# Attention scores and sums on TensorE: products of both kinds dealt out one by one, half a unit later

## The reference

```python
q = conv1x1(wq, x).reshape(n, NH, HD, H, W)      # NH = 16 heads, HD = 16; k and v alike
qk = einsum('nhcij,nhciw->nhijw', q, k) / D      # D = 16
qrq = einsum('nhcij,chjw->nhijw', q, rq) / D
krk = einsum('nhcij,chjw->nhijw', k, rk) / D
weight = softmax(qk + Gq * qrq + Gk * krk, axis=3)
out = einsum('nhijw,nhciw->nhcij', weight, Gv1 * v) + einsum('nhijw,chjw->nhcij', weight, Gv2 * rv)
return conv1x1(wo, out)
```

## Time and profile before

| what | us |
|---|---|
| median of three runs | 8297.43 |
| the profiled execution | 8291.75 |
| its span, first to last instruction | 8290.0 |
| PE, mean granted clock over the span | 0.749 |
| POOL normalise (L787), mean of one | 1.934 |
| DVE add and largest (L737), mean of one | 0.286 |

### The profile page before, as it was taken

The page is one execution under the profiler, slowest core; times in us unless marked ns, Lnnn a source line. Parts: engine busy times, 40 slices in busy tenths (PEclk is TensorE's granted clock), DMA queues, the critical chain, the costliest instruction groups (busy, mean ns, idle before and its releaser), DMA issues. The chain is left out here.

```text
span 8290.0 us, 275612 instructions
## 1 busy us (share of the span) xinstructions
PE 7187.2 (87%) x106442; PEld 6044.4 (73%) x106442; DVE 5176.6 (62%) x20646; ACT 4856.3 (59%) x11427; POOL 2457.0 (30%) x1235
## 2 busy tenths in 40 slices
PE   4999999799999999999999899999999966766738
PEld 3555555689988888898899898898888932332338
DVE  5444444366666666666666666666666768988830
ACT  1444444577777777777777777777777733333410
POOL 0000000243443443444434444434434432322210
PEclk7999999666666666666666666666667688988855
DMA  7555555565655665655556656656656576766522
GB/s 217 203 203 204 204 204 197 113 112 100 112 103 98 113 107 101 107 99 107 101 106 112 102 100 109 109 99 110 105 100 109 92 232 203 265 201 202 208 74 99
DMA packets 1721071, 1148.11 MB, mean 138 GB/s; under 512 B 1143009, under 2 KB 1506145, under 8 KB 1703329
## 3 DMA queue, kind: packets, MB, share of 16 engines
q1 hardware_dynamic: 1530336, 842.56, 48.1%
q10 hardware_dynamic: 188352, 285.27, 9.3%
q0 software_dynamic: 1024, 2.09, 0.1%
HBM read 708.04 MB, written 421.56 MB: 136 GB/s over the span
## 5 line engine op out<-in xcount | busy, mean ns | idle before, releaser
L787 POOL TENSOR_TENSOR att_scores<-att_scores,att_inverse 128x1024 f32<-128x1024 f32 x1024 | 1966.8, 1934 | 2951.7 <-DVE att_inverse L722 2951.7
L660 ACT ACTIVATE att_scores<-att_scores,att_negmax 128x128 f32<-128x128 f32 x8192 | 2509.2, 399 | 67.6 <-issue 67.6
L737 DVE CUSTOM_DVE_ANT_0 att_scores<-att_ps,att_scores 128x128 f32<-128x128 f32 x8192 | 1780.8, 286 | 1066.7 <-PE att_ps L573 957.5
L560 PE MATMUL att_ps<-att_qk,att_rs 32*128 32x64 f32 x32768 | 1793.2, 380 | 155.6 <-ACT att_scores L652 114.2
L560 PEld LDWEIGHTS att_ps<-att_qk,att_rs 32*128 32x128 f32 x32768 | 1698.6, 299 | 196.2 <-ACT att_scores L652 142.5
L573 PE MATMUL att_ps<-att_own 16*128 16x128 f32 x16384 | 1541.6, 405 | 231.3 <-issue 224.1
L573 PEld LDWEIGHTS att_ps<-att_own 16*128 16x128 f32 x16384 | 1416.2, 300 | 268.9 <-issue 264.4
L652 ACT ACTIVATE att_scores<-att_ps 128x1024 f32<-128x1024 f32 x1024 | 992.4, 1021 | 1044.3 <-PE att_ps L560 1044.3
L720 DVE TENSOR_REDUCE att_total<-att_scores 128x8 f32<-128x1024 f32 x1024 | 1233.7, 1205 | 70.7 <-issue 70.7
L594 PE MATMUL att_ps<-att_scores,att_rv 128*16 128x64 f32 x32768 | 1249.6, 334 | 11.0 <-issue 10.8
L594 PEld LDWEIGHTS att_ps<-att_scores,att_rv 128*16 128x16 f32 x32768 | 1193.6, 127 | 24.5 <-issue 13.1
(11 more groups left out here) (146 smaller groups left out, 5276.0 us busy)
## 6 DMA issues: line engine op xcount, KB each, us to landing
qk<-proj_qk_out ACTq DMA_DIRECT2D x64, 2048.0 KB, 8.5
att_qk<-qk SPq DMA_DIRECT2D x512, 256.0 KB, 6.7
att_own<-qk SPq DMA_DIRECT2D x2048, 64.0 KB, 2.5
proj_x<-in_x_dram SPq DMA_DIRECT2D x128, 512.0 KB, 4.3
v_t<-proj_v_out ACTq DMA_DIRECT2D x64, 1024.0 KB, 11.3
att_vt<-v_t SPq DMA_DIRECT2D x128, 512.0 KB, 5.5
att_v<-att_att_v SPq DMA_DIRECT2D x512, 128.0 KB, 4.2
att_r<-att_att_r SPq DMA_DIRECT2D x512, 128.0 KB, 3.5
```

Source lines behind the costliest of these rows:

```text
L560: last = pe.matmul(ps[:, 4 + g, jj * IU:(jj + 1) * IU], rs[32 * g:32 * g + 32, t * JB + jj, :], qk[b][32 * g:32 * g + 32, :, t * JB + jj], ...
L660: last = act.activation(scores[v][:, i, :], scores[v][:, i, :], ACT.Exp, bias=negmax[v][:, i:i + 1], scale=-1.0)
L737: last = dve.tensor_tensor_reduce(out=scores[v][:, i, :], in0=ps[:, 2 * (p % 2) + r // 4, (r % 4) * W:(r % 4 + 1) * W], in1=scores[v][:, i ...
L787: pool.tensor_tensor(scores[v][:, rows, :], scores[v][:, rows, :], inverse[v][:, rows].unsqueeze(2).broadcast_to([P, PR, W]), ALU.mult).th ...
```

## The change

Only `attend` and constants above it are changed. In words:

- PE deals its products out one by one. A unit has four quarters. In each step a few own products, a few table products and a few sums follow each other.
- Everything is shifted by half a unit: in the first half of unit u the sums are those of the second half of unit u - 2, in the second half those of the first half of u - 1. In the last quarter the table products are round 0 of unit u + 2.
- Own scores come in 16 pieces of four image rows, two pieces (two row groups) together, in every second group of steps. They take 32 array rows instead of 16, of which the lower half is cleared once to zero. They use banks 0 and 1; the table products 2 to 5; sums with v bank 6; sums with rv bank 7.
- ACT no longer reads v; DVE reads all four fills. ACT and DVE follow with pieces of four rows; sums, inverses and normalising stay at eight rows.
- vt, att_v and att_r are halved into two buffers each, with their own semaphores; rv comes in four loads. Loads and stores are issued in halves or quarters. att_r is laid out in runs of 16 instead of 32 in DRAM, and `combine` reads it so.

```diff
-PR = 8
+PR = 4
 PIECES = IU // PR
+SR = 8
+SPIECES = IU // SR
-JT = JG
+JT = JG // 2
+STORES_G = JG // JT
...
+            def own_score(u, p, r):
+                half, g = p // (PIECES // 2), p % G
+                if r == 0:
+                    if p % (PIECES // 2) == 0:
+                        pe.wait_ge(own_loaded[half], 128 * u + 128)
+                    later(pe, added, PIECES * u + p - 1)
+                at = (p // G) % (HROWS // 16) * PR + r
+                last = pe.matmul(ps[:, p % 2, r * W:(r + 1) * W], own[half][32 * g:32 * g + 32, 1, at, :], own[half][32 * g:32 * g + 32, 0, at, :],
+                                 start=True, stop=True, tile_position=(32 * g, 0))
...
+            def unit(u, v, parts):
+                back2, back1, now, ahead1, ahead2 = parts
+                for q in range(4):
+                    rel_on, sums_on = (ahead1, ahead1, ahead1, ahead2)[q], (back2, back2, back1, back1)[q]
+                    ru, rt = (u + 1, q + 1) if q < 3 else (u + 2, 0)
+                    rb = v + 1 if q < 3 else v + 2
+                    su, sb, b = (u - 2, v - 2, q + 2) if q < 2 else (u - 1, v - 1, q - 2)
+                    for x in range(PR):
+                        if now:
+                            own_score(u, 4 * q, x)
+                            own_score(u, 4 * q + 1, x)
+                        if rel_on:
+                            relative(ru, rb, rt, range(3 * x, 3 * x + 3))
+                        if sums_on:
+                            sums_with_v(su, sb, b, range(2 * x, 2 * x + 2))
+                    for x in range(PR):
+                        if rel_on:
+                            relative(ru, rb, rt, range(12 + 3 * x, 15 + 3 * x))
+                        if sums_on:
+                            sums_with_v(su, sb, b, range(8 + 2 * x, 10 + 2 * x))
+                            sums_with_r(su, sb, b, range(2 * x, 2 * x + 2))
+                    for x in range(PR):
+                        if now:
+                            own_score(u, 4 * q + 2, x)
+                            own_score(u, 4 * q + 3, x)
+                        if rel_on:
+                            relative(ru, rb, rt, range(24 + 2 * x, 26 + 2 * x))
+                        if sums_on:
+                            sums_with_r(su, sb, b, range(8 + 2 * x, 10 + 2 * x))
+                    for x in range(PR):
+                        if sums_on:
+                            sums_with_r(su, sb, b, range(16 + 4 * x, 20 + 4 * x))
...
             def unit(u, v, parts):
                 back2, back1, now, ahead1, ahead2 = parts
+                for p in range(PIECES):
+                    if p < BEHIND:
+                        if back1:
+                            exp_piece(u - 1, (v - 1) % BUFS, PIECES - BEHIND + p)
+                    elif now:
+                        exp_piece(u, v, p - BEHIND)
+                    q = p // 4
+                    if p % 4 == 3:
+                        if q < 3 and ahead1:
+                            read_relative(u + 1, v + 1, q + 1)
+                        if q == 3 and ahead2:
+                            read_relative(u + 2, v + 2, 0)
+                        if q < 2 and back2:
+                            read_r(u - 2, q + 2)
+                        if q >= 2 and back1:
+                            read_r(u - 1, q - 2)
```

More of the change, by code:

```diff
@@ L512, in unit @@
                     load_qk(*after(h, k, 2))
-                fresh = left >= 2 and k == UPH - 2
+                if started >= 2:
+                    store(*before(h, k, 2), u - 2, 0)
+                if started >= 1:
+                    ph, pk = before(h, k, 1)
+                    later(sp, v_done, FILLS * (u - 2) + FILLS // 2)
+                    load_v(ph, pk, 0)
+                    if pk == 0:
+                        later(sp, r_done, FILLS * (u - 2) + FILLS // 2)
+                        load_rv(ph, 0)
+                        load_rv(ph, 1)
+                fresh = k == UPH - 2 and left >= 2
                 if fresh:
@@ L520, in unit @@
                     load_own(*after(h, k, 1), 0)
+                if started >= 1:
+                    later(sp, v_done, FILLS * (u - 1))
+                    load_v(ph, pk, 1)
+                    if pk == 0:
+                        later(sp, r_done, FILLS * (u - 1))
+                        load_rv(ph, 2)
+                        load_rv(ph, 3)
+                if started >= 2:
+                    store(*before(h, k, 2), u - 2, 1)
                 if fresh:
@@ L546, in _ @@
+            store(NH - 1, UPH - 2, UNITS - 2, 1)
+            for a in range(2):
+                store(NH - 1, UPH - 1, UNITS - 1, a)
+            for a in range(2):
+                sp.wait_ge(v_stored[a], 64 * UNITS)
+                sp.wait_ge(r_stored[a], 64 * UNITS)
         @block.tensor
         def _(pe):
[L548 to L596, removed]
@@ new lines, in relative @@
+            def relative(u, v, t, steps):
+                if 0 in steps:
+                    if t == 0:
+                        pe.wait_ge(qk_loaded[v % 2], 64 * (u // 2) + 64)
+                    if t % (ROUNDS // 2) == 0:
+                        pe.wait_ge(rs_ready[t // (ROUNDS // 2)], u // UPH + 1)
+                    later(pe, rel_read, ROUNDS * u + t)
+                for x in steps:
+                    jj, g = x // G, x % G
+                    last = pe.matmul(ps[:, 2 + g, jj * IU:(jj + 1) * IU], rs[32 * g:32 * g + 32, t * JB + jj, :],
+                                     qk[v % 2][32 * g:32 * g + 32, :, t * JB + jj], start=True, stop=True, tile_position=(32 * g, 0))
+                if JB * G - 1 in steps:
+                    last.then_inc(rel_done, 1)
@@ new lines, in sums_with_v @@
+            def sums_with_v(u, v, b, steps):
+                if 0 in steps:
+                    if b % (FILLS // 2) == 0:
+                        pe.wait_ge(v_loaded[b // (FILLS // 2)], 16 * u + 16)
+                    if b == 0:
+                        pe.wait_ge(normed, SPIECES * u + SPIECES)
+                    later(pe, v_read, FILLS * u + b)
+                for x in steps:
+                    r, g = x // G, x % G
+                    i = 16 * b + 4 * r + g
+                    last = pe.matmul(ps[32 * g:32 * g + HD, 6, r * W:(r + 1) * W], vt[i // HROWS][:, i % HROWS, :], scores[v % BUFS][:, i, :],
+                                     start=True, stop=True, tile_position=(0, 32 * g))
+                if 15 in steps:
+                    last.then_inc(v_done, 1)
@@ new lines, in sums_with_r @@
+            def sums_with_r(u, v, b, steps):
+                if 0 in steps:
+                    pe.wait_ge(rv_loaded[b], (u // UPH) * 16 + 16)
+                    later(pe, r_read, FILLS * u + b)
+                for x in steps:
+                    jj, g = x // G, x % G
+                    j = g * JG + b * JB + jj
+                    last = pe.matmul(ps[32 * g:32 * g + HD, 7, jj * IU:(jj + 1) * IU], rv[:, j, :], scores[v % BUFS][:, :, j],
+                                     start=True, stop=True, tile_position=(0, 32 * g))
+                if JB * G - 1 in steps:
+                    last.then_inc(r_done, 1)
@@ L640, in _ @@
+            pe.wait_ge(cleared, 3)
             for t in range(ROUNDS):
-                relative(0, 0, t)
+                relative(0, 0, t, range(JB * G))
+            relative(1, 1, 0, range(JB * G))
             units(pe, unit)
@@ new lines, in read_r, with unit @@
+            def read_r(u, b):
+                act.wait_ge(r_done, FILLS * u + b + 1)
+                if b % 2 == 0:
+                    later(act, r_stored[b // 2], 64 * u)
+                act.activation(att_r[b // 2][:, :, (b % 2) * JB:(b % 2 + 1) * JB], ps[:, 7, :].rearrange("p (j i) -> p i j", i=IU), ACT.Copy).then_inc(r_read, 1)
+            BEHIND = 2
+            def unit(u, v, parts):
+                back2, back1, now, ahead1, ahead2 = parts
+                for p in range(PIECES):
[14 more added lines that the diff above has]
+                            read_r(u - 1, q - 2)
@@ new lines, in _, with unit @@
+            BEHIND = 2
+            def unit(u, v, parts):
+                back2, back1, now, ahead1, ahead2 = parts
+                for p in range(PIECES):
+                    q = p // 4
+                    if now:
+                        add_and_largest(u, v, p)
+                    if p % 4 == 2 and q < 2 and back2:
+                        read_v(u - 2, q + 2)
+                    if p % 4 == 2 and q >= 2 and back1:
+                        read_v(u - 1, q - 2)
+                    if p % 2 == 1:
+                        k = p // 2 - BEHIND
+                        if k >= 0 and now:
+                            sums_of(u, v, k)
+                        elif k < 0 and back1:
+                            sums_of(u - 1, (v - 1) % BUFS, SPIECES + k)
@@ L773, in _ @@
+            for half in range(2):
+                dve.memset(own[half][:, :, :, :], 0.0).then_inc(cleared, 1)
```

(9 more changed lines are left out.)

221 lines of the change are left out of this document (53 added, 168 removed).

## The result

The changed kernel takes 11,529.76 us (median of 4 runs, 11,481.67 to 11,549.69) against 8,293.69: ratio 1.389, 95% interval 1.3845 to 1.3944. 12,700 was forecast: the change was to cost about 4,400 us and costs 3,236. All of it is in the attention stage.

The account below looks back on a forecast made before the run. PE (TensorE), busy 4,709 of attention's 5,086 us, was taken as the bound. 8,292 + 4,400 (74.1 us a unit, 128 units, half clock) + 40 for part units = 12,730, said as 12,700; 8 in 10: 8,200 to 13,400.

Parts of the forecast that it names:

- What a change of kind costs: On PE in attention, each switch between row and column products costs 0.09 us at full, 0.14 at half clock; 96 against 2.
- A: Quarter's section, four steps of 2 own, 3 table, 2 v products; step's rows 0.99 us, columns 0.56 at half clock.
- B: Quarter's section, four steps of 3 table, 2 v, 2 rv products; step's rows 0.57 us, columns 0.81 at half clock.
- C: Quarter's section, four steps of 2 own, 2 table, 2 rv products; step's rows 0.83 us, columns 0.39 at half clock.
- section D: Last section of a quarter on PE, 16 rv products in all, nothing but sums; 1.16 us at half clock.
- Rivals 2 and 3: Changes of kind cost nothing between short runs: 7,180 us in total (chance 0.17), or with the clock down 8,300 (0.06).
- The added wait: PE waits at each quarter's start for ACT to read four table banks: 0.8 us four times, 3.1 a unit.
- Which clock: PE in attention stays at half clock throughout: 74.1 us a unit, 9,485 us instead of 5,086, +4,400.
- What costs nothing: ACT and DVE work, smaller pieces, 32-row own scores, clearing, loads and combining add 0; part units at the ends about +40 us.
- the case of half of the time up: Rival: changes of kind cost as forecast, but full clock half of the time, about 11,100 us; chance 0.17 with clock always up.

Follow-up runs that it names:

- by section: The changed kernel with sections A, B and C of a quarter each making row products first, column products after (24 changes of kind a unit, not 96): 8,197 us, ratio 0.989.

## Why the prediction was right, and where it was not

- **What a change of kind costs: right.** It was read off three seams of the kernel before, and the changed kernel shows the same gaps behind 128-column records. The parts of a step came out, at half clock, at 1.05 and 0.55 us for A (0.99 and 0.56 forecast), 0.63 and 0.76 for B (0.57 and 0.81), 0.89 and 0.33 for C (0.83 and 0.39); at full clock 0.64, 0.33, 0.41, 0.55, 0.53 and 0.32 (0.60, 0.31, 0.36, 0.51, 0.51, 0.29). At half clock the row parts of A, B and C are each 0.06 longer than forecast: the prediction took 0.25 for the seam from table products to sums, and it is 0.33. Added up with section D and the wait, the measured parts make about 75 us a unit at half clock (74.1 forecast) and 53 at full (49.1). Rivals 2 and 3, that a change costs nothing between short runs, are refuted by the trace and by the four orders.
- **The added wait: right in size by luck, wrong in its cause.** The first step of a quarter takes 2.00 us for its rows at half clock (median) against 1.05 for the others: 0.95, forecast 0.8. But PE does not wait for ACT's reads of the table products there. It waits for DVE, in its second own piece, which needs the bank that DVE has not yet read. The end of a quarter and the start of the next in the changed kernel, by engine:

```profile
5003.12 1.49 PE L620 MATMUL att_ps<-att_scores,att_rv 128*16 128x64 f32 x36
5004.54 0.79 PE L593 MATMUL att_ps<-att_own 32*128 32x128 f32 x2
5005.65 0.37 PE L593 MATMUL att_ps<-att_own 32*128 32x128 f32 x1 [0.32 <-DVE att_negmax L739]
5005.74 0.37 PE L581 MATMUL att_ps<-att_qk,att_rs 32*128 32x64 f32 x2
...
5003.24 1.94 ACT L673 ACTIVATE att_scores<-att_ps 128x1024 f32<-128x1024 f32 x2 [7.40 <-PE att_ps L581]
...
5005.51 0.08 DVE L739 DVE_READ_ACCUMULATOR2_ANT att_negmax<- 128x1 f32 x1
```

  ACT has read the tables at 5005.18, DVE ends with the last own piece of the old quarter at 5005.59, and PE's second own piece starts at 5005.65, with the table products behind it in PE's order. In 482 of 511 quarters that piece starts 0.05 to 0.06 us after this DVE instruction, ACT mostly having ended 0.3 us before. The prediction had put DVE's waits at nothing. ACT's reads come next: by an estimate from these times they alone would have held PE back about 0.3 us less.
- **Which clock: the step that failed.** I took half clock throughout because a mixed stretch had far fewer sum records per us than the stretches ahead of a rise. That counted section D in the average and passed over that it is a stretch of nothing but sums, 36 records in 1.42 us: 25 a us, just the rate that the prediction gives for the stretch ahead of a rise. Half clock throughout is 12,700, and the two kernels that stay near it (0.52 and 0.50) take 12,724 and 12,941. The changed kernel does not: it is at full clock for a third of the time. The measured time lies just inside the forecast's own range of 11,450 to 13,500, and that is luck: the lower end stood for no added wait and overlapping sections, and neither came about. The upper end was added up wrongly, too: 81 us a unit make 13,600.
- **The term behind it** is under "What costs nothing": own scores from 32 rows, "the columns streamed are the same, so 0". For PE's own time that is so (shown); for the clock it is worth 1,194 us here. With 16 rows the forecast would have been off by 0.2%. I had named the clock as the bound of this edit and put 0.17 on all cases in which it stays up; the case of half of the time up, about 11,100, is the near one.
- **The two pages.** The rule of the Trainium skill ("TensorEngine Tiling (Array Packing)", Tiling Modes) that a change of mode drains the engine was the one to go by; the gaps above agree. The rule of the Trainium skill ("TensorE: Matmul & The Clock Gate", Part 1) on idle gaps was not enough: the stretches at 0.50 above have PE busy 10.00 of 10.00 us, and with 16 rows for 32 the clock falls from 0.67 to 0.52 with the same order and waits. It is not refuted for the fall in the kernel before: there the clock goes down right behind the 1.14 us in which PE waits for ACT, and no run tells this wait from the row products as its cause.
- **What costs nothing** otherwise held: the other stages take 8 us less together, and ACT (3,667 us) and DVE (3,472 us) are busy for less than half of the stage's 8,346. DVE still holds PE back once a quarter, as told above. At the changes of head the tables came late (8.6 us, found by section); in the changed kernel PE is so slow that it hardly shows.

## What to carry to other kernels

Deal out products finely only if they use the same tiles of the array; price each change between row groups and column groups from a seam of your own trace, and count the changes. Where TensorE runs at half clock though it is busy, look at which products fill the time: with short runs of products on all 128 rows between those on 32 rows it was 0.89 here for 0.68, and the kernel took 8,197 us against 8,295 in spite of 22 extra changes, though only together with the zero rows (8,356 without). That kernel has the shift by half a unit as well, whose share is not known. When an edit "costs nothing", ask it twice, once for the engine and once for its clock. And do not take the size of a wait for proof of whom it is for: look up which instruction ended last ahead of it.

## What the runs showed that I had not expected

Rows of zeros count for the clock: 16 more array rows in one product of six, all zero, moved the granted clock of the stage from 0.52 to 0.67 and the kernel by 1,194 us. A run of 36 sum records in 1.4 us raised the clock some 360 times in the changed kernel and 95 times with own scores from 16 rows. Why the one depends on the other stays open.
